# Dropping three of GpSimd's four pacing waits in a message layer, and moving an attention score from TensorE's table to VectorE

## The chip, the cores and the metric

The kernel runs on one core of a Trainium2 chip. The metric is the time of one execution on the device in microseconds. The core has five engines with instruction queues of their own: TensorE (PE, with its weight loads shown as PEld), VectorE (DVE), ScalarE (ACT), GpSimd (POOL), and SyncE (SP), which here only issues transfers. Engines wait for each other by semaphores alone.

## The reference, cut to what matters

Two graph layers over 12,500 nodes with 32 features each, with a layer norm after each. The first layer has 400,000 edges, the second is computed in this kernel over the same edge list.

```
# layer 0, per edge e (source node src[e], target dst[e]):
x    = silu(edge_radial @ W1 + b1)          # 8 -> 64
x    = silu(x @ W2 + b2)                    # 64 -> 64
tpw  = x @ W3 + b3                          # 64 -> 256, four 8x8 blocks per edge
m0   = a * (sum_u hs[src] sh0 W00 + sum_u,i hv[src] sh1 W110 / sqrt(3))
m1   = a * (sum_u hs[src] sh1 W01 + sum_u hv[src] sh0 W10)
agg  = segment_sum(concat(m0, m1), dst) / 4
x    = layernorm(x + h_self + agg)

# layer 1:
s_src, s_dst = x @ attn_w[:32], x @ attn_w[32:]
e     = leaky_relu(s_src[src] + s_dst[dst], 0.01)
alpha = exp(e - segment_max(e)) / segment_sum(exp(...))
x     = layernorm(x + segment_sum(x[src] * alpha, dst))
```

## The kernel before, in words

Edges are sorted by target. Edge number p*3125 + t lies on partition p, column t; a "tile" is one column t of 128 edges.

**The message stage** (about the first 4,700 us) goes over 130 iterations of 24 tiles. An iteration has four groups k = 0..3 (`SLOTS`) of 6 tiles; groups 0 and 1 are half 0, groups 2 and 3 are half 1. All engines run the same loop, two iterations unrolled, each in the order in which its instructions are written; there is no planner.

- TensorE, for each group g: the third layer of g (`layer3`, L595, 6 matmuls into one of two PSUM banks `tpw`, ends with `tpw_ready`), the second layer of g+1 (`layer2`, L585), after k = 1 and k = 3 a one-hot product that fetches one tile's node rows from a table in SBUF (`find_tile`, L604, 14 matmuls), and the first layer of g+2 (`layer1`, L581, ends with `layers_done`). So TensorE is two groups ahead of VectorE.
- ScalarE, for each group: silu after the second layer (`hidden`, L685), at k = 0 and 2 a copy of the gathered rows (`spread_hv`, L698), the one-hots for `find_tile` (L707, L710), some counting work for the first 101 iterations, and last silu after the first layer of g+2 (`first_hidden`, L679, waits for `layers_done`).
- VectorE: two products of the third layer's output with the gathered rows (`product_a`, L953, and `product_b`, L962, which ends with `tpw_used`), their reductions, and the previous iteration's scaling (L992 once per iteration) and scan.
- GpSimd: `gather_again` issues one indirect DMA for each tile whose node rows come from HBM: 6 for k = 0, 5 for k = 1, 6 for k = 2, 5 for k = 3 (L475, tile name `early<-in_x_wide,idx`). In the first 101 iterations one more follows, `gather_dst_row` (`dst_row`). They fill the row slots of the next iteration. What a slot must wait for is `tpw_used`: VectorE is done with that slot's rows. The function has a second wait beside it:

```
pool.wait_ge(tpw_used, it * SLOTS + k - 1)
if k % HALF == 0:
    pool.wait_ge(tpw_ready, it * SLOTS + k - 1)
else:
    pool.wait_ge(layers_done, it * SLOTS + k)
```

That is: before groups 0 and 2 also for TensorE's third layer of the group two before the one gathered for, counted in TensorE's order, and before groups 1 and 3 for the first layer. SyncE refills the inputs and loads the next indices once the gathers of both halves have landed.

**The attention stage** (from about 4,960 to 8,180 us) goes over 125 blocks of 25 tiles. For 17 of them (`GT1`) GpSimd gathers rows of 33 floats (32 features and the score `s_src`) from a table in HBM, `gather_block`; before every fourth gather it waits for `found_ready` of a tile of TensorE's. The other 8 tiles (`PT`) TensorE fetches: `find_rows`, L662, 8 tiles x 7 node batches x 2 splits (the table as high part and low part), each a 128x128 one-hot against `BC` = 14 x 33 = 462 columns. VectorE then picks one of the 14 nodes by a mask product (`keep_one`, L1268) and a reduction (L1276) into `ring`, makes the one-hots for the next block (L1253), and runs the softmax with running maximum (`softmax_block`). All 33 columns, the score among them, come out of the product; `ring[:, k, :, D]` is the score that L1287 reads.

Of the kernel before, what the change touches and what calls it, by code (L numbers as in the profile page):

```python
# [5 lines left out]
ALU = mybir.AluOpType  # L6
ACT = mybir.ActivationFunctionType
AX = mybir.AxisListType.X
# [5 lines left out]
P = 128  # L14
# [37 lines left out]
PA = GT * MUL * 3 * MUL  # L52
GT1 = BT - PT
PC = PT * P
BC = BJ * TW
CHUNKS = ((0, (PT + 1) // 2), ((PT + 1) // 2, PT))
SPLITS = 2
ROUND = 12582912.0
# [20 lines left out]
def build(nc, x, x_wide, x_t, src, src_pe, src_rows, src_pex, src_rowsx, dst, dst_firsts, dst_edges, sh, radial_t, w1, b1, w2, b2, w3, b3, w_self,  # L79
# [17 lines left out]
    with ExitStack() as ctx:  # L97
# [6 lines left out]
        def sem(name):  # L104
            return ctx.enter_context(nc.semaphore(name))
# [53 lines left out]
        def msgs(m, tiles):  # L159
# [70 lines left out]
        picked_at = run_at + run_size  # L230
        picked = [prod_f[:, picked_at + i * BC:picked_at + (i + 1) * BC].rearrange("p (w a) -> p w a", a=BJ)
                  for i in range(2)]

        with ExitStack() as first:
            def sb1(name, shape, dt=F32):
# [12 lines left out]
        with ExitStack() as second:  # L248
            def sb2(name, shape, dt=F32):
                return second.enter_context(nc.sbuf_tensor(name, shape, dt))  # L250

            lows = sb2("lows", [P, NJ * TW], F32R)
            highs = sb2("highs", [P, NJ * TW], F32R)
            hot_f = sb2("hot", [P, NBATCH * PC], F32R)

        xs = xs_f[:, NJ * (TW - D):NJ * TW].rearrange("p (j d) -> p j d", d=D)
# [68 lines left out]
        splits_ready, hot_ready = sem("splits_ready"), [sem(f"hot_ready{i}") for i in range(2)]  # L325
        found_ready, found_used = sem("found_ready"), sem("found_used")
        mask_ready, picked_ready = sem("mask_ready"), sem("picked_ready")
        run_ready, run_stored = sem("run_ready"), [sem(f"run_stored{i}") for i in range(2)]

        decay_ready = sem("decay_ready")  # L330
# [142 lines left out]
        def _(pool):  # L473
# [13 lines left out]

            def gather_again(it, k, m, loads, all_tiles=False):
                pool.wait_ge(tpw_used, it * SLOTS + k - 1)
                if k % HALF == 0:  # L490
                    pool.wait_ge(tpw_ready, it * SLOTS + k - 1)
                else:
                    pool.wait_ge(layers_done, it * SLOTS + k)
                if k == 0:
                    pool.wait_ge(idx_in[m], loads * 16 + 16)
                pool.nop(nofuse=True)
                gather_tiles(m, k, all_tiles)
# [340 lines left out]
        def _(dve):  # L838
# [376 lines left out]
            for b in range(NBATCH):  # L1215
                js = slice(b * BJ, (b + 1) * BJ)
                dve.wait_ge(batch_in[0][b], 16 * BJ)
                link(dve.tensor_tensor(vv[0], agg0[0:P, js, :], bc(has_w[0:P, js]), ALU.mult))
                link(dve.tensor_tensor(vv[1], vv[0], xs[0:P, js, :], ALU.add))
                link(layernorm(h1[0:P, js, 0:D]))  # L1220
                for a, dest in ((0, h1[0:P, js, D:TW].rearrange("p j o -> p (j o)")), (1, tval[0:P, js])):
                    link(dve.tensor_tensor(
                        vv[2], h1[0:P, js, 0:D],
                        attns[0:P, a * D:(a + 1) * D].unsqueeze(1).to_broadcast([P, BJ, D]), ALU.mult))
                    link(dve.tensor_reduce(dest, vv[2], AX, ALU.add))
                dve.sem_inc(h1_ready, 1)
                whole = h1[:, js, :].rearrange("p j w -> p w j")
                hi, lo = (split(s, b).rearrange("p (w j) -> p w j", j=BJ) for s in range(SPLITS))
                link(dve.tensor_copy(hi, whole))
                dve.tensor_tensor(lo, whole, hi, ALU.subtract).then_inc(splits_ready, 1)  # L1230
# [15 lines left out]
            def one_hot(b, n, k, c):  # L1246

                first_tile, end_tile = CHUNKS[c]
                if c == 0:
                    dve.wait_ge(qb_in[k], n * 16 + 16)  # L1250
                dve.wait_ge(found_ready, b * PT + end_tile)
                for g in range(NBATCH):
                    ins = dve.tensor_scalar(hot(c)[:, g, :], qb[k][:, first_tile * P:end_tile * P],  # L1253
                                            slot_of[:, g:g + 1], None, ALU.is_equal)
                ins.then_inc(hot_ready[c], 1)

            def pick(b, n, k):

                edges = bass.ds(b * PT, PT)
                dve.tensor_tensor(mask[:, k, :, :], amod[:, edges].unsqueeze(2).to_broadcast([P, PT, BJ]),  # L1260
                                  iota.unsqueeze(1).to_broadcast([P, PT, BJ]), ALU.is_equal).then_inc(mask_ready, 1)
                dve.wait_ge(mask_ready, b + 1)

                def keep_one(i):
                    dve.wait_ge(found_ready, b * PT + PT + i + 1)
                    if i > 1:
                        dve.wait_ge(picked_ready, b * PT + i - 1)
                    dve.tensor_tensor(picked[i % 2], found[i][:, 0:BC].rearrange("p (w a) -> p w a", a=BJ),  # L1268
                                      mask[:, k, i:i + 1, :].to_broadcast([P, TW, BJ]), ALU.mult).then_inc(found_used, 1)

                keep_one(0)
                for i in range(PT):
                    if i + 1 < PT:
                        keep_one(i + 1)
                    dve.wait_ge(found_used, b * PT + PT + i + 1)
                    dve.tensor_reduce(ring[:, k, GT1 + i, :], picked[i % 2], AX, ALU.add).then_inc(picked_ready, 1)  # L1276
                    if i + 1 == CHUNKS[0][1]:
                        one_hot(b + 1, n + k, 1 - k, 0)
                one_hot(b + 1, n + k, 1 - k, 1)

            def softmax_block(b, pair, k):
                n = b * BLOCK_STEPS
                edges = bass.ds(b * BT, BT)
                top = run[:, k, :, SW - 1]
                dve.wait_ge(ring_in[k], pair * (16 * GT1) + 16 * GT1)
                dve.wait_ge(picked_ready, b * PT + PT)
                dve.tensor_tensor(score[:, 0, :], ring[:, k, :, D], filled[:, edges], ALU.add)\  # L1287
                   .then_inc(block_step, 1)
                dve.wait_ge(block_step, n + 1)
                dve.scalar_tensor_tensor(out=score[:, 1, :], in0=score[:, 0, :], scalar=0.01,  # L1290
                                         in1=score[:, 0, :], op0=ALU.mult, op1=ALU.max)\
                   .then_inc(block_step, 1)

                dve.wait_ge(block_step, n + 2)
                dve.wait_ge(run_stored[k], pair * 16 + 16)
                dve.wait_ge(row0_ready, b + 1)
                dve.tensor_tensor_scan(top[:, 1:], pen[:, edges], score[:, 1, :], top[:, 0:1],
                                       ALU.add, ALU.max).then_inc(block_step, 1)

                dve.wait_ge(block_step, n + 3)  # L1300
                dve.tensor_tensor(diff[:, 0, :], top[:, 0:BT], pen[:, edges], ALU.add)\
                   .then_inc(block_step, 1)
                dve.tensor_tensor(diff[:, 1, :], score[:, 1, :], top[:, 1:], ALU.subtract)\  # L1303
                   .then_inc(block_step, 1)
                dve.wait_ge(block_step, n + 4)
                dve.tensor_tensor(diff[:, 0, :], diff[:, 0, :], top[:, 1:], ALU.subtract)\
                   .then_inc(block_step, 1)
                dve.wait_ge(exp_ready, b + 1)
                for f in range(0, D, MUL):
                    ins = dve.tensor_tensor(acc[:, f:f + MUL, :].rearrange("p f t -> p t f"),  # L1310
                                            acc[:, D, :].unsqueeze(2).to_broadcast([P, BT, MUL]),
                                            ring[:, k, :, f:f + MUL], ALU.mult)
                ins.then_inc(ring_used, 1)
                dve.tensor_copy(run[:, 1 - k, 0, SW - 1:SW], run[:, k, BT, SW - 1:SW]).then_inc(row0_ready, 1)
                dve.wait_ge(ring_used, b + 3)
                dve.wait_ge(decay_ready, b + 1)
                first = acc[:, :, 0]
                dve.scalar_tensor_tensor(out=first, in0=got[1 - k][:, :, BT - 1], scalar=enter1[:, :], in1=first,
                                         op0=ALU.mult, op1=ALU.add).then_inc(added, 1)
                dve.wait_ge(added, b + 1)  # L1320
                for f in range(0, TW, PART):
                    part = slice(f * BT, min(f + PART, TW) * BT)
                    ins = dve.tensor_tensor_scan(got_f[k][:, part], decay_f[:, part], acc_f[:, part], 0.0,
                                                 ALU.mult, ALU.add)
                ins.then_inc(scanned1, 1)
# [132 lines left out]
```

## Time and profile before

| | |
|---|---|
| Times of three runs | 8414.13, 8416.13, 8420.86 us; median 8416.13 |
| Profiled execution | span 8423.6 us, its own time 8425.42 us |
| Busy over the span | PE 80%, PEld 62%, DVE 77%, ACT 33%, POOL 64% |
| Mean granted TensorE clock | 0.888 of full speed |
| DMA | 363 MB in 318,658 packets, 43 GB/s over the span |

The ends of TensorE's matmuls in a profile are modelled from their size; the starts are recorded. A busy share says little by itself here, since the two stages have different limits: the rows below are read by stage.

### The profile page before, as it was taken

To read this page: it belongs to the slowest core of one execution; us is meant where nothing else is said; L and a number is where in the kernel's file an instruction comes from. 1 tells how busy PE (TensorE), PEld (TensorE's weight loads), DVE (VectorE), ACT (ScalarE), POOL (GpSimd) and SP (SyncE) were. 2 spreads that over 40 slices of the span, in tenths; PEclk is the share of its full clock that TensorE was granted. 3 is DMA by queue.
4 is the path that set the end of the run, shared out by engine and by line. 5 is a ranking of instruction groups with operands and counts; after the bars stand their busy time and mean duration, and the time that the engine had idled before them with its cause. 6 is when DMAs were issued, how large, how long until landed. Compare 5 with 4: busy or idle time off the path is not lost.

```text
span 8423.6 us, 93644 instructions
## 1 busy us (share of the span) xinstructions
PE 6705.5 (80%) x26126; PEld 5191.3 (62%) x26126; DVE 6512.7 (77%) x11130; ACT 2820.1 (33%) x4982; POOL 5375.5 (64%) x5400
## 2 busy tenths in 40 slices
PE   6777777777777777777777508999999999999992
PEld 4555555555555555555555407888888888888881
DVE  7888877888878787888787537878787788787874
ACT  4555555555545545544444201111111111111110
POOL 5666666666656666666565566666666666666666
PEclk8888888888888888888888659999999999999996
DMA  2222122222222211211111202222222222222221
GB/s 62 42 41 42 40 41 42 42 42 41 41 39 42 41 41 38 42 39 35 34 33 32 48 18 47 50 51 48 48 53 48 48 48 53 48 48 53 48 48 27
DMA packets 318658, 363.23 MB, mean 43 GB/s; under 512 B 157447, under 2 KB 259511, under 8 KB 317963
## 3 DMA queue, kind: packets, MB, share of 16 engines
q0 software_dynamic: 175840, 136.07, 12.2%
q1 hardware_dynamic: 142794, 226.94, 8.4%
q14 instruction: 19, 0.15, 0.0%
q8 instruction: 5, 0.08, 0.0%
HBM read 251.38 MB, written 111.20 MB: 43 GB/s over the span
## 4 chain that ended last, share of the span: by engine, by line
PE 59%; issue 16%; another core or an unknown queue 9%; DVE 8%; ACT 6%; POOL 1%; DMA 1%; ACTq 0%; DVEq 0%; SPq 0%; POOLq 0%
PE tpw L662 26%; PE tpw L595 12%; PE hid L662 8%; PE hid L604 4%; PE hid L585 4%; PE hid L581 4%; ACT early L685 2%; ACT nearx L707 1%; POOL msgs L475 1%; ACT hid L679 1%; DVE early L974 1%; DVE prod L962 1%; DVE msgs L1023 1%; DVE prod L953 1%
## 5 line engine op out<-in xcount | busy, mean ns | idle before, releaser
L475 POOL DMA_INDIRECT early<-in_x_wide,idx x2870 | 2803.5, 977 | 1793.9 <-issue 1724.5
L475 POOL DMA_INDIRECT prod<-table,idx x2125 | 2180.5, 1026 | 1023.1 <-issue 597.1
L662 PE MATMUL tpw<-highs,hot 128*128 128x462 f32 x5250 | 1993.8, 380 | 78.1 <-issue 62.1
L662 PE MATMUL tpw<-lows,hot 128*128 128x462 f32 x5250 | 1979.3, 377 | 50.9 <-issue 50.3
L595 PE MATMUL tpw<-w3s,early 128*128 128x256 f32 x6252 | 1842.4, 455 | 6.9 <-issue 6.9
L595 PEld LDWEIGHTS tpw<-w3s,early 128*128 128x128 f32 x6252 | 1384.4, 229 | 575.5 <-issue 341.9
L662 PEld LDWEIGHTS tpw<-highs,hot 128*128 128x128 f32 x5250 | 1007.2, 192 | 234.7 <-issue 107.0
L662 PEld LDWEIGHTS tpw<-lows,hot 128*128 128x128 f32 x5250 | 1002.1, 191 | 186.1 <-issue 75.4
L685 ACT ACTIVATE early<-hid,b2s 64x384 f32<-64x384 f32 x1042 | 601.5, 577 | 1008.9 <-PE hid L585 570.1
L581 PE MATMUL hid<-early,w1s 16*128 16x384 f32 x1044 | 546.3, 607 | 485.3 <-ACT early L685 410.0
L585 PE MATMUL hid<-hid,w2s 128*128 128x384 f32 x1042 | 499.2, 563 | 500.2 <-ACT hid L679 274.0
L604 PE MATMUL hid<-x_highs,hotx 128*128 128x448 f32 x1792 | 770.2, 430 | 116.5 <-DVE pickedx L1053 114.1
L815 ACT ACTIVATE big<-diff 128x25 f32<-128x25 f32 x125 | 28.1, 225 | 2384.9 <-DVE diff L1303 1018.0
L935 DVE TENSOR_TENSOR bprod<-hv,sh 128x288 f32<-128x288 f32 (+1 forms) x261 | 121.8, 467 | 891.9 <-ACT hv L698 582.5
L1253 DVE TENSOR_SCALAR hot<-big,bases 128x512 fp32r<-128x512 f32 x1764 | 725.1, 482 | 0.2 <-DVE prod L1243 0.2
L953 DVE TENSOR_TENSOR prod<-tpw,early 128x1152 f32<-128x1152 f32 x521 | 700.3, 1344 | 24.3 <-remote 24.1
L604 PE MATMUL hid<-x_lows,hotx 128*128 128x448 f32 x1792 | 700.5, 391 | 0.0
L962 DVE TENSOR_TENSOR prod<-tpw,hv 128x1152 f32<-128x1152 f32 x521 | 700.1, 1344 | 0.0
L1268 DVE TENSOR_TENSOR prod<-tpw,mask 128x462 f32<-128x462 f32 x750 | 467.6, 637 | 274.7 <-remote 158.3
L662 PE MATMUL hid<-highs,hot 128*128 128x462 f32 x1750 | 656.7, 375 | 9.8 <-issue 9.7
L662 PE MATMUL hid<-lows,hot 128*128 128x462 f32 x1750 | 652.6, 373 | 7.5 <-issue 7.4
L581 PEld LDWEIGHTS hid<-early,w1s 16*128 16x128 f32 x1044 | 170.9, 204 | 737.4 <-issue 476.7
(186 smaller groups left out, 8729.0 us busy)
## 6 DMA issues: line engine op xcount, KB each, us to landing
big<-qrows SPq DMA_DIRECT2D x126, 512.0 KB
scan<-prod SPq DMA_DIRECT2D x125, 425.0 KB
scan<-sums SPq DMA_DIRECT2D x130, 384.0 KB
early<-in_x_wide,idx POOLq DMA_INDIRECT x2870
prod<-table,idx POOLq DMA_INDIRECT x2125
qbx<-qx SPq DMA_DIRECT2D x131, 128.0 KB
early<-in_radial_t SPq DMA_DIRECT2D x262, 48.0 KB
sh<-in_sh SPq DMA_DIRECT2D x131, 48.0 KB
```

The source lines that it names most:

```text
L475: return pool.indirect_dma_start(out=dest, out_offset=None, in_=source, in_offset=bass.IndirectOffsetOnAxis(ap=index, axis=0))
L581: pe.matmul(hid[:, 0, 0:HC], w1s[:, :], rad[:, k, :], start=True, stop=True).then_inc(layers_done, 1)
L585: pe.matmul(hid[:, 0, 0:HC], w2s[:, :], hid1[:, :], start=True, stop=True).then_inc(layer2_done, 1)
L595: mm = pe.matmul(tpw_v(b)[:, t, :], hid2[:, b, at:at + P], w3s[:, :], start=True, stop=True)
L604: mm = pe.matmul(hid[:, 1, 0:BX], hotx[m][:, g, h * P:(h + 1) * P], x_split(s, g), start=g == 0 and s == 0, stop=g == NBATCH - 1 and s == ...
L662: mm = pe.matmul(found[i][:, 0:BC], hot(c)[:, g, at:at + P], split(s, g), start=g == 0 and s == 0, stop=g == NBATCH - 1 and s == SPLITS - 1)
L685: ins = act.activation(hid2[0:HR, b, half * HC:(half + 1) * HC], hid[units, 0, 0:HC], ACT.Silu, bias=b2s[units, :])
L935: dve.tensor_tensor(bprod[:, 0:tiles, :, :], hv[:, h, 0:tiles, :].rearrange("p t (i u) -> p t i u", i=3), sh1.rearrange("p o i t -> p (o t ...
L953: dve.tensor_tensor(prod_a[b].rearrange("p (t w u) -> p t w u", t=GT, w=MUL), w[:, :, 0:3 * MUL * MUL].rearrange("p t (w u) -> p t w u", w ...
L962: dve.tensor_tensor(prod_b[b].rearrange("p (t i w u) -> p t i w u", t=GT, i=3, w=MUL), w[:, :, 3 * MUL * MUL:].rearrange("p t (w u) -> p t ...
L1253: ins = dve.tensor_scalar(hot(c)[:, g, :], qb[k][:, first_tile * P:end_tile * P], slot_of[:, g:g + 1], None, ALU.is_equal)
L1268: dve.tensor_tensor(picked[i % 2], found[i][:, 0:BC].rearrange("p (w a) -> p w a", a=BJ), mask[:, k, i:i + 1, :].to_broadcast([P, TW, BJ]) ...
```

## The change

Two edits that have nothing to do with each other.

In the message stage GpSimd's second wait stays for k = 0 alone, with the same value as before; for k = 1, 2 and 3 only the wait for `tpw_used` is left.

In the attention stage TensorE's node table and its products have 32 columns per node instead of 33 (462 columns become 448). The score of the 8 tiles that TensorE fetches is computed by VectorE instead: after the eighth tile is picked, one product of the 8 x 32 picked features with the attention weights and one sum over the 32 features, written into column `D` of the ring. The softmax block waits for that (`found_scored`) in place of `picked_ready`. The table in HBM and GpSimd's gathers keep 33 columns.

```diff
-BC = BJ * TW
+BC = BJ * D
...
+        by_attn_at = picked_at + 2 * BC
+        by_attn = prod_f[:, by_attn_at:by_attn_at + PT * D].rearrange("p (t d) -> p t d", d=D)
+        assert by_attn_at + PT * D <= 4 * PA
...
-            highs = sb2("highs", [P, NJ * TW], F32R)
+            highs = sb2("highs", [P, NJ * D], F32R)
...
+        by_attn_ready, found_scored = sem("by_attn_ready"), sem("found_scored")
...
             def gather_again(it, k, m, loads, all_tiles=False):
                 pool.wait_ge(tpw_used, it * SLOTS + k - 1)
-                if k % HALF == 0:
-                    pool.wait_ge(tpw_ready, it * SLOTS + k - 1)
-                else:
-                    pool.wait_ge(layers_done, it * SLOTS + k)
+                if k == 0:
+                    pool.wait_ge(tpw_ready, it * SLOTS - 1)
                 if k == 0:
                     pool.wait_ge(idx_in[m], loads * 16 + 16)
                 pool.nop(nofuse=True)
...
-                whole = h1[:, js, :].rearrange("p j w -> p w j")
+                whole = h1[:, js, 0:D].rearrange("p j w -> p w j")
...
                     dve.tensor_tensor(picked[i % 2], found[i][:, 0:BC].rearrange("p (w a) -> p w a", a=BJ),
-                                      mask[:, k, i:i + 1, :].to_broadcast([P, TW, BJ]), ALU.mult).then_inc(found_used, 1)
+                                      mask[:, k, i:i + 1, :].to_broadcast([P, D, BJ]), ALU.mult).then_inc(found_used, 1)
...
-                    dve.tensor_reduce(ring[:, k, GT1 + i, :], picked[i % 2], AX, ALU.add).then_inc(picked_ready, 1)
+                    dve.tensor_reduce(ring[:, k, GT1 + i, 0:D], picked[i % 2], AX, ALU.add).then_inc(picked_ready, 1)
...
                 one_hot(b + 1, n + k, 1 - k, 1)
+                dve.wait_ge(picked_ready, b * PT + PT)
+                dve.tensor_tensor(by_attn, ring[:, k, GT1:, 0:D],
+                                  attns[:, 0:D].unsqueeze(1).to_broadcast([P, PT, D]), ALU.mult).then_inc(by_attn_ready, 1)
+                dve.wait_ge(by_attn_ready, b + 1)
+                dve.tensor_reduce(ring[:, k, GT1:, D], by_attn, AX, ALU.add).then_inc(found_scored, 1)
...
-                dve.wait_ge(picked_ready, b * PT + PT)
+                dve.wait_ge(found_scored, b + 1)
                 dve.tensor_tensor(score[:, 0, :], ring[:, k, :, D], filled[:, edges], ALU.add)\
                    .then_inc(block_step, 1)
```

## Rows read from the trace of the kernel before

**Rows 1.** The page's chain that ended last, shares by engine.
```profile
PE 59%; issue 16%; another core or an unknown queue 9%; DVE 8%; ACT 6%; POOL 1%; DMA 1%; ACTq 0%; DVEq 0%; SPq 0%; POOLq 0%
```

**Rows 2.** Windows: stretch, its length, busy us (instructions) by engine, clock, DMA.
```profile
200.00:4500.00 4300.00, 3313.99 (x10975) 2272.32 (x10974) 3468.65 (x4297) 2175.22 (x4062) 2650.51 (x2715) 0.87 0.20 40
5500.00:8000.00 2500.00, 2391.62 (x11007) 2094.57 (x11007) 2010.11 (x4817) 353.38 (x441) 1712.19 (x1672) 0.98 0.23 50
```

**Rows 3.** Waits, whole span: us in total, times, longest us.
```profile
ACT hid L679 <- remote: 703.7, 135, 7.8
DVE bprod L935 <- ACT hv L698: 582.5, 150, 9.1
```

**Rows 4.** Timeline of one message iteration: start us, us, instruction [idle before <-releaser].
```profile
3015.66 0.95 POOL L475 DMA_INDIRECT early<-in_x_wide,idx  x1 [4.91 <-issue]
...
3024.17 1.35 DVE L962 TENSOR_TENSOR prod<-tpw,hv 128x1152 f32<-128x1152 f32 x1
...
3025.41 0.91 PE L581 MATMUL hid<-early,w1s 16*128 16x384 f32 x2
...
3028.30 0.95 POOL L475 DMA_INDIRECT early<-in_x_wide,idx  x1 [0.30 <-issue]
...
3030.58 1.33 DVE L962 TENSOR_TENSOR prod<-tpw,hv 128x1152 f32<-128x1152 f32 x1
3031.21 0.58 ACT L679 ACTIVATE hid<-hid,b1s 128x384 f32<-128x384 f32 x1 [7.39 <-remote]
...
3032.06 0.95 POOL L475 DMA_INDIRECT early<-in_x_wide,idx  x1 [2.81 <-issue]
...
3050.74 0.95 POOL L475 DMA_INDIRECT early<-in_x_wide,idx  x1 [3.52 <-issue]
```

**Rows 5.** Timeline of two later iterations without a pause before k = 2.
```profile
4027.34 0.95 POOL L475 DMA_INDIRECT early<-in_x_wide,idx  x1 [9.79 <-issue]
...
4066.19 0.94 POOL L475 DMA_INDIRECT early<-in_x_wide,idx  x1 [9.91 <-issue]
...
4390.29 0.95 POOL L475 DMA_INDIRECT early<-in_x_wide,idx  x1 [8.04 <-issue]
...
4400.99 0.58 ACT L679 ACTIVATE hid<-hid,b1s 128x384 f32<-128x384 f32 x1 [2.86 <-issue]
...
4418.35 0.95 POOL L475 DMA_INDIRECT early<-in_x_wide,idx  x1 [0.30 <-issue]
...
4421.54 1.36 DVE L953 TENSOR_TENSOR prod<-tpw,early 128x1152 f32<-128x1152 f32 x1 [2.95 <-remote]
...
4430.65 0.94 POOL L475 DMA_INDIRECT early<-in_x_wide,idx  x1 [11.35 <-issue]
```

**Rows 6.** Line L992, in every second iteration: first and last start.
```profile
L992 DVE TENSOR_TENSOR early<-early,sh x65: 947/949/987, 126.8 to 4738.8; 128x768 f32<-128x768 f32 x65
```

**Rows 7.** Pieces of the chain: back-to-back matmuls of 462 and of 448 columns.
```profile
3043.28 2.81 PE hid L604 x14
...
5105.57 17.72 PE tpw L662 x84
```

**Rows 8.** Groups by line and form: busy us, mean ns, idle before.
```profile
L1276 DVE TENSOR_REDUCE prod<-prod 128x33 f32<-128x462 f32 x1000 | 613.6, 624 | 0.0
L1268 DVE TENSOR_TENSOR prod<-tpw,mask 128x462 f32<-128x462 f32 x750 | 467.6, 637 | 274.7 <-remote 158.3 <-PE hid L662 55.6 <-PE tpw L662 29.2
L1053 DVE TENSOR_TENSOR pickedx<-hid,maskx 128x448 f32<-128x448 f32 x256 | 157.6, 616 | 0.0
L1061 DVE TENSOR_REDUCE early<-pickedx 128x32 f32<-128x448 f32 x256 | 155.5, 608 | 0.0
L935 DVE TENSOR_TENSOR bprod<-hv,sh 128x288 f32<-128x288 f32 x260 | 121.5, 467 | 891.9 <-ACT hv L698 582.5 <-issue 234.7 <-DMA sh<-in_sh 74.4
L475 POOL DMA_INDIRECT early<-in_x_wide,idx x2870 | 2803.5, 977 | 1793.9 <-issue 1724.5 <-PE hid L581 31.1 <-DVE prod L962 19.0
L475 POOL DMA_INDIRECT prod<-table,idx x2125 | 2180.5, 1026 | 1023.1 <-issue 597.1 <-remote 185.1 <-PE tpw L662 181.6
```

## The prediction

> **What bounds the kernel now.** I read the chain that ended last first. TensorE has 59% of it, and 9% is "another core or an unknown queue", odd on a single core [rows 1]. The windows then part two stages. In the message stage no engine is full: over 4,300 us VectorE is busy 3,469, TensorE 3,314, and the clock is 0.87. In the attention stage TensorE is: 2,392 of 2,500 us at clock 0.98 [rows 2]. There 11,007 matmuls at 112 a block are 98.3 blocks, 25.44 us each, of which VectorE is idle (2,500 - 2,010) / 98.3 = 5.0 us.
>
> The waits say what the odd 9% is: ScalarE's L679 waits 703.7 us for "remote", 135 times, 5.2 us each, about once per iteration [rows 3]. L679 waits only for TensorE's first layer. The timeline of one iteration shows it. TensorE's first layer (L581) starts at 3025.41 and takes 0.91, so it is over at 3026.32. But ScalarE's L679 starts at 3031.21, and GpSimd's gather before k = 2, which waits for the third layer that follows L581, at 3032.06 [rows 4]. Nothing else releases them: TensorE's signals arrive late, that of the first layer by 4.9 us, and together. When do they come? GpSimd had issued 11 gathers from 3015.66 to 3028.30 + 0.95 = 3029.25; L679 starts 1.96 us after that. I went through the timeline of all iterations with L581 and L679 side by side: of 127, L679 is late by more than 4 us in 90, again about 1.9 us after the last gather of the run, and on time in 37 (of the first 99, which have `gather_dst_row`, 78 late and 21 on time; of the last 28, 12 and 16). Signals given in the first five gathers of a run are on time, those given after the eighth mostly late, those after the eleventh nearly always. I take it as this kernel's rule, without knowing its cause: while GpSimd issues indirect DMAs back to back, TensorE's signals get stuck after about 10 us and come out when the run has drained. So the pauses in GpSimd's run are worth something, and the change removes the one before k = 2.
>
> **Message stage.** Before groups 1 and 3 the removed wait ends no idle time: gathers follow each other at 1.25 us. The value for k = 0 is unchanged. What counts is k = 2: GpSimd idles 3032.06 - 3029.25 = 2.81 us there [rows 4]. Without that wait, k = 2 needs VectorE's third `product_b` counted from that run's iteration, started 3024.17, over at 3025.52, and k = 3 the one started 3030.58, over at 3031.91. GpSimd reaches k = 2 at 3015.66 + 11 x 1.25 = 3029.4 and k = 3 at 3036.9. Both are met, so the two runs of 11 and 12 gathers become one of 23 (22 after iteration 100). That lasts 28.75 us from the start S of the run, and the drain ends at S + 28.75 + 1.9 = S + 30.65.
>
> The trace has two such runs, where the wait before k = 2 happened to be met in time: from 4027.34 and 4390.29. They go without a pause, the second to 4418.35 + 0.95. Start of run to start of next is 38.85 and 40.36 us, against 35.08 for 3015.66 to 3050.74 [rows 4, 5], and 36.0 us mean: 128 iterations from 126.8 to 4738.8 [rows 6]. In both L679 was on time (4400.99), but the third layer's signal was then stuck until the drain, and VectorE's L953 waited until 4421.54, 2.2 us after the last gather [rows 5]. So a merged run costs (38.85 + 40.36) / 2 - 36.0 = 3.6 us where L679 is on time, and 1.25 more for the 23rd gather: 4.9.
>
> Where L679 is late, it is stuck from S + 10.7 on. Before, release to next run start was 3050.74 - 3031.2 = 19.6 us: second layer, silu, `spread_hv`, VectorE's products, the third layer that k = 0 waits for. That stretch now begins at S + 30.65, so the iteration takes 50.2 us, +14.2 (22 gathers: 49.0, +13.0). VectorE, idle from S + 16.3, covers nothing.
>
> Behind GpSimd's waits only gathers are queued, and who waits for them (`spread_hv`) is not waiting for their landing now. So an earlier landing gives 0; at most the 2.81 us before k = 2 could come back each iteration, 360 us.
>
> Which of the two cases? I keep the shares of now, since S and what TensorE and VectorE do after it keep their order: 78 x 14.2 + 21 x 4.9 + 12 x 13.0 + 16 x 3.6 = 1,108 + 103 + 156 + 58 = 1,425 us. Bounds: all on time 99 x 4.9 + 28 x 3.6 = 586; all late 99 x 14.2 + 28 x 13.0 = 1,770.
>
> The Trainium skill, Perfetto Trace Analysis, in its section on what the profiler's window captures for TensorE, says that a matmul's end is computed from its size, and that the signal is pushed only when PSUM has acknowledged the write. By that rule the gap between 3026.32 and 3031.21 could be matmuls that really ended late, and GpSimd would have no part in it; that is the second rival below. Rows 4 and 5 speak against it: the same matmuls let L679 go at once in the iteration of 4400.99, at the same place in the run (10.7 us after its start).
>
> **Attention stage.** TensorE: 84 matmuls of 462 columns take 17.72 us, 0.2110 each, and 14 of 448 columns 2.81, 0.2007 [rows 7]. That saves 0.0103 x 112 = 1.15 us a block, 144 us if TensorE alone set the pace. VectorE: eight products fall from 637 to 616 ns and eight reductions from 624 to 608, 0.30 us less [rows 8]; a product and a reduction of 256 elements are added. No row has that size; the product of 288 takes 467 [rows 8], so two at up to 0.47, and two handovers of about 0.1: +1.1, net +0.8 us. It lies after the picks and before the softmax, in 5.0 us of idle time a block. If that cover were gone it would cost 0.8 x 125 = 100 us. GpSimd: 17 gathers at 1.026 + 0.30 are 22.5 us a block [rows 8], about what TensorE's block becomes (112 x 0.2007 = 22.5), so the engines touch, and GpSimd's pauses for `found_ready` shrink with the faster tiles, which lets its runs grow. Half of the gain: -70 us, between -144 and +100. The splits of the table are seven shorter copies ahead of the stage, and narrower operands there are worth under 1 us.
>
> GpSimd's gathers take 1,026 ns here and 977 in the message stage [rows 8]. The Trainium skill, GPSIMD Engine Reference, Key points, gives a reason that speaks against the change: GpSimd shares its SBUF interfaces with VectorE, and a VectorE instruction with two SBUF inputs contends with it. The added product is one. By that rule a gather could be held up by 0.47 us, 58 us in 125 blocks, inside the bound above.
>
> **The sum.** The profiled execution's own time is 8425.4 us (span 8423.6). + 1,425 - 70 = 9,780. That execution is 9.3 above the median of 8416.13, so 9,770.
>
> **Rivals.**
> 1. Mild: the long run shifts the phase so that L679 is on time as in the two natural cases. For it: both natural long runs were on time, and so was the run after them. Against: in the first 99 iterations 79% are late. Time: 8,416 + 586 - 70 = 8,930.
> 2. The late signals have nothing to do with the length of GpSimd's run, only with `find_tile` ahead of them. Then the merged run costs nothing and attention gives its 70 to 144, perhaps with part of the 2.81 us an iteration: 8,416 - 70 = 8,350, down to about 8,000. For it: each late signal follows the 14 matmuls, and the two natural long runs are only two. Against: the release follows the end of the gathers, not that of the matmuls. This is the other side; it decides if L679 starts under 5 us after L581 in the new trace although the run goes on.
> 3. The pauses don't go: `product_b` comes later than GpSimd in the new steady state, so `tpw_used` splits the run by itself. Then the message stage stays within +-1 us an iteration; with attention 8,220 to 8,480. Against: margins of 3.9 and 5.0 us [rows 4].
>
> **How the numbers follow.** Forecast 0.60 (9,400 to 10,150 of its own), mild 0.23 (8,700 to 9,300), rival 2 0.11, rival 3 0.06. Two executions of this kernel differ by up to 0.08%, so 0.2% (17 us) can be told from no change. Faster by more: rival 2 and half of 3, 0.13. Within: 0.02. Slower: 0.85. The range leaves out the faster side and the very top: 8,700 to the all-late bound, 8,416 + 1,770 + 100 = 10,290.
>
> **What would show it.** Right: GpSimd's idle time before the seventh to twelfth gather gone; runs of 22 and 23; L679's wait for "remote" near 20 us a time in most iterations; intervals of L992 of 50 and 41 us; TensorE's clock in the message stage below 0.87, as it idles; a step of 0.20 us for L662 and blocks near 24.9 us. Wrong: L679 released in the middle of a run; runs still split before k = 2; intervals under 37 us.

## The result and the profile after

The changed kernel takes 9817.78 us (median of 4 runs, 9802.88 to 9851.71) against 8415.13 for the kernel before (4 runs, 8413.39 to 8420.86). The ratio is 1.167, with a 95% interval of 1.164 to 1.170: slower by a sixth, 48 us above the forecast of 9,770.

The chain that ended last, in the page of the changed kernel, answers to [rows 1]:

```profile
PE 46%; issue 20%; another core or an unknown queue 19%; DVE 8%; ACT 5%; DVEq 0%; ACTq 0%; DMA 0%; SPq 0%
```

"Another core or an unknown queue" was 9% and is 19%, on a single core. The windows, with the columns of [rows 2], say in which stage:

```profile
200.00:4500.00 4300.00, 2530.87 (x8403) 1725.16 (x8402) 2658.63 (x3299) 1695.42 (x3190) 2037.23 (x2104) 0.79 0.16 31
7000.00:9300.00 2300.00, 2145.49 (x9981) 1919.11 (x9980) 1873.29 (x4542) 320.41 (x401) 1557.17 (x1517) 0.97 0.23 49
```

In the message stage each engine runs 21 to 23% fewer instructions in the same 4,300 us, and the clock falls from 0.87 to 0.79. In the attention stage 9,981 matmuls are 89.1 blocks of 112, 25.8 us each, where they were 25.4. So almost the whole loss is in the message stage. From the first to the last matmul of the third layer it takes 6,070.5 us instead of 4,712.7, which is +1,358 of the 1,402 between the two profiled executions. The attention stage, measured the same way, is 3,219.0 instead of 3,175.2, and the remaining 536 us are unchanged within 1 us.

One iteration shows how. Timeline of the changed kernel, columns of [rows 4]; L583 is TensorE's first layer, L587 the second, L681 and L687 are ScalarE's silus behind them (L679 and L685 before):

```profile
2973.69 0.95 POOL L479 DMA_INDIRECT early<-in_x_wide,idx  x1 [14.32 <-PE tpw L597]
...
2983.45 0.91 PE L583 MATMUL hid<-early,w1s 16*128 16x384 f32 x2
...
2987.57 0.95 POOL L479 DMA_INDIRECT early<-in_x_wide,idx  x1 [0.30 <-issue]
...
2999.24 0.58 ACT L681 ACTIVATE hid<-hid,b1s 128x384 f32<-128x384 f32 x1 [17.40 <-remote]
2999.88 1.65 PE L587 MATMUL hid<-hid,w2s 128*128 128x384 f32 x2 [12.74 <-issue]
...
3001.33 0.94 POOL L479 DMA_INDIRECT dst_row<-in_dst,row_i  x1 [0.31 <-issue]
3006.39 1.17 ACT L687 ACTIVATE early<-hid,b2s 64x384 f32<-64x384 f32 x2 [6.56 <-remote]
...
3008.17 0.46 DVE L937 TENSOR_TENSOR bprod<-hv,sh 128x288 f32<-128x288 f32 x1 [18.22 <-ACT hv L700]
...
3025.81 0.95 POOL L479 DMA_INDIRECT early<-in_x_wide,idx  x1 [23.53 <-issue]
```

GpSimd issues its 23 gathers from 2973.69 to 3002.27 without a pause; the gather at 2987.57, the twelfth, had 2.81 us of idle time ahead of it before. TensorE's first layer is over at 2984.36 (2983.45 + 0.91). Its signal reaches ScalarE at 2999.24, 14.9 us later. The second layer is over at 3001.53, and its signal reaches L687 at 3006.39, 4.9 us later and 4.1 after the last gather. Then comes the stretch that no gather covers, until the third layer releases the next run. The iteration takes 52.1 us. The second layer's 1.65 us are a price of the idle time as well: TensorE had stood still for 12.74 us, and windows around the two places give its granted clock in the column behind POOL, full (2.4 GHz) at 2983.4 and half (1.2 GHz) at 2998.5:

```profile
2983.40:2984.40 1.00, 1.00 (x4) 0.41 (x4) 1.00 (x3) 0.00 (x0) 0.70 (x1) 1.00 0.19 23
...
2998.50:3001.60 3.10, 1.65 (x2) 0.50 (x2) 0.00 (x0) 0.58 (x1) 2.18 (x4) 0.50 0.12 16
```

Waits over the whole span, columns of [rows 3]:

```profile
POOL early L479 <- issue: 2245.6, 2800, 25.2
DVE bprod L937 <- ACT hv L700: 1788.3, 202, 18.3
ACT early L687 <- remote: 1187.9, 118, 16.4
ACT hid L681 <- remote: 890.9, 56, 22.3
```

L681 is late less often than L679 was (56 of these waits instead of 135) but by 15.9 us instead of 5.2. The second silu, which before had 54 such waits of 5.5 us on average, has 118 of 10.1 us.

### The profile page after: what moved, and what is told of

Read it like the earlier page. It is cut to its first block, busy times and chain, and to the rows that moved or that the text cites. A ratio compares the mean times of both kernels' runs of the same rounds, so it can differ in the third digit from the quotient of the medians.

```text
span 9825.9 us, 93830 instructions
## 1 busy us (share of the span) xinstructions
PE 6667.5 (68%) x26126; PEld 5203.4 (53%) x26126; DVE 6578.7 (67%) x11380; ACT 2820.0 (29%) x4982; POOL 5365.7 (55%) x5400
## 4 chain that ended last, share of the span: by engine, by line
PE 46%; issue 20%; another core or an unknown queue 19%; DVE 8%; ACT 5%; DVEq 0%; ACTq 0%; DMA 0%; SPq 0%
PE tpw L664 21%; PE hid L664 7%; PE tpw L597 7%; PE hid L606 6%; PE hid L587 3%; PE hid L583 2%; ACT early L687 2%; ACT nearx L709 2%; DVE early L976 1%; ACT hid L681 1%; DVE pickedx L1055 1%; ACT hv L700 1%; DVE hot L1255 1%; DVE early L945 1%
## 5 line engine op out<-in xcount | busy, mean ns | idle before, releaser
L479 POOL DMA_INDIRECT prod<-table,idx x2125 | 2187.6, 1029 | 1058.2 <-issue 585.9
L664 PE MATMUL tpw<-highs,hot 128*128 128x448 f32 x5250 | 1946.0, 371 | 51.4 <-issue 32.5
L664 PE MATMUL tpw<-lows,hot 128*128 128x448 f32 x5250 | 1951.4, 372 | 40.2 <-issue 39.9
L597 PE MATMUL tpw<-w3s,early 128*128 128x256 f32 x6252 | 1787.4, 444 | 8.4 <-issue 7.1
L597 PEld LDWEIGHTS tpw<-w3s,early 128*128 128x128 f32 x6252 | 1349.5, 223 | 576.7 <-issue 357.5
L583 PE MATMUL hid<-early,w1s 16*128 16x384 f32 x1044 | 570.3, 631 | 1358.9 <-ACT early L687 703.6
L587 PE MATMUL hid<-hid,w2s 128*128 128x384 f32 x1042 | 535.2, 600 | 970.6 <-issue 616.8
L687 ACT ACTIVATE early<-hid,b2s 64x384 f32<-64x384 f32 x1042 | 601.6, 577 | 1984.7 <-remote 1187.9
L583 PEld LDWEIGHTS hid<-early,w1s 16*128 16x128 f32 x1044 | 179.5, 214 | 1632.7 <-issue 1489.9
L587 PEld LDWEIGHTS hid<-hid,w2s 128*128 128x128 f32 x1042 | 196.6, 214 | 1098.0 <-issue 657.4
L664 PE MATMUL hid<-lows,hot 128*128 128x448 f32 x1750 | 679.6, 388 | 62.6 <-issue 62.5
L664 PE MATMUL hid<-highs,hot 128*128 128x448 f32 x1750 | 676.0, 386 | 67.5 <-issue 66.8
```

The source lines that it names most:

```text
L479: return pool.indirect_dma_start(out=dest, out_offset=None, in_=source, in_offset=bass.IndirectOffsetOnAxis(ap=index, axis=0))
L583: pe.matmul(hid[:, 0, 0:HC], w1s[:, :], rad[:, k, :], start=True, stop=True).then_inc(layers_done, 1)
L587: pe.matmul(hid[:, 0, 0:HC], w2s[:, :], hid1[:, :], start=True, stop=True).then_inc(layer2_done, 1)
L597: mm = pe.matmul(tpw_v(b)[:, t, :], hid2[:, b, at:at + P], w3s[:, :], start=True, stop=True)
L664: mm = pe.matmul(found[i][:, 0:BC], hot(c)[:, g, at:at + P], split(s, g), start=g == 0 and s == 0, stop=g == NBATCH - 1 and s == SPLITS - 1)
L687: ins = act.activation(hid2[0:HR, b, half * HC:(half + 1) * HC], hid[units, 0, 0:HC], ACT.Silu, bias=b2s[units, :])
```

## Experiments

Each run is told by its edit against the changed kernel, and timed beside the kernel before on the same chip. "Stage" is the message stage as above.

**The two halves of the change, each alone.** First the waits with the 33 columns of before, then the columns with the waits of before:

```diff
 # e1: the changed waits, BC = BJ * TW and the score by TensorE as before
 # e2: the changed columns, and
-                if k == 0:
-                    pool.wait_ge(tpw_ready, it * SLOTS - 1)
+                if k % HALF == 0:
+                    pool.wait_ge(tpw_ready, it * SLOTS + k - 1)
+                else:
+                    pool.wait_ge(layers_done, it * SLOTS + k)
```

> The kernel before with GpSimd's waits as in the changed one, TensorE's table still 33 columns wide. Theory (merged runs of gathers hold TensorE's signals back): all of the loss in the message stage is here. The changed trace has its message stage 1,358 us longer, so 8,415 + 1,358 = 9,770 to 9,780, with iterations of 50 to 52 us alternating with 42 to 44. If the columns or the new VectorE work in the attention stage were part of the message stage's loss by some coupling: under 9,700.

> The 32-column table and the score by VectorE alone, GpSimd's waits as before. Message stage as before (36.0 us an iteration). Attention stage: the changed trace has it 44 us longer (3,219 against 3,175 us), against the predicted 70 us shorter. If that holds by itself: 8,455 to 8,465. If the attention stage's loss came from anything the message stage left behind (phase, clock): 8,345 to 8,415.

Measured: e1 9810.27 us beside 8420.11, ratio 1.165 (1.162 to 1.168), stage 6,029 us. e2 8427.95, ratio 1.0009 (1.0000 to 1.0018), stage 4,660 us. The waits are the whole loss: e1 came out 30 us above its forecast. The columns are worth nothing that can be told from zero: +8 us, 0 to +15. That lies between the two bands given for e2, so it decides for neither. In its trace the message stage is 52 us shorter than in the trace of the kernel before, though the code of that stage is the same, and the attention stage 44 us longer. The kernel before has no trace from this chip, so how the +8 divides between the stages is open.

**Which of the waits removed.** The third layer's before k = 2 put back, then the first layer's before k = 1 and k = 3 instead:

```diff
 # e3
-                if k == 0:
-                    pool.wait_ge(tpw_ready, it * SLOTS - 1)
+                if k % HALF == 0:
+                    pool.wait_ge(tpw_ready, it * SLOTS + k - 1)
 # e4, beside the wait for k == 0
+                if k % HALF == 1:
+                    pool.wait_ge(layers_done, it * SLOTS + k)
```

> The changed kernel with the wait for the third layer back for k = 2 as well; only the waits for the first layer (k = 1 and 3) are gone. Theory: the pause before k = 2 is the one that counts, runs of 11 and 12 return, and the time is that of the columns alone, about 8,460, ratio to before 1.003 to 1.008. Rival (the odd groups' waits also hold something up): above 8,600.

> The changed kernel with the waits for the first layer (k = 1 and 3) back, the one for the third layer before k = 2 still gone. Theory: k = 2 starts at once, so the run goes to 17 gathers; the signal that k = 3 waits for (the first layer given after about 18 us in the run) is itself late, so GpSimd stops there after 17 gathers, the run drains, and the signals come out at S + 17 x 1.25 + 1.9 = S + 23.2 instead of S + 30.65. Late iterations about 50.2 - 7.4 = 43 us plus the second run's share, on-time ones 38 to 40: 41 us mean, 8,415 + 5 x 127 + 44 = about 9,100. Rival (the odd waits do nothing, they are met before): 9,820 as the changed kernel.

Measured: e3 8435.54, ratio 1.0017 (1.0008 to 1.0026), below its band of 1.003 to 1.008; its runs are of 11 and 12 gathers again, but for two of 22. e4 9277.14, ratio 1.102 (1.099 to 1.104); its runs are of 17 and 6, or of 5, again but for two of 22. So the wait before k = 2 is the one that counts. e4 came out 2% above its forecast. The time follows the longest run: 12 gathers 8,436, 17 gathers 9,277, 23 gathers 9,810.

**Is it the wait for TensorE, or the pause?** Here GpSimd waits for its own gathers to land, and for nothing that TensorE does:

```diff
 # e5
+                if k == 2:
+                    pool.wait_ge(rows_in[0], rows_until(it))
 # e6: that, and before k = 1 and k = 3
+                if k % HALF == 1:
+                    pool.wait_ge(rows_in[k // HALF], rows_until(it) - 16 * (GT if all_tiles else GT - 1))
```

> The changed kernel with a pause of another kind before k = 2: GpSimd waits until its own gathers for k = 0 and 1 have landed, and for nothing of TensorE's. Theory (signals are held while GpSimd gathers back to back, whoever ends the run): runs of 11 and 12 with a pause of about 2.4 us, first-layer signal released as before, 36 us an iteration, 8,410 to 8,450. Rival (it is TensorE's wait itself, the order it forces, that kept the stage fast, for instance by keeping GpSimd from running ahead): near 9,800.

> The changed kernel with such a pause before k = 1, 2 and 3: runs of 6, 5, 6 and 5 (6 with dst_row), none past 7.5 us. Theory: no signal is ever held, ScalarE's L679 starts at once in all iterations, the 5 us wait goes; GpSimd needs 23 x 1.25 + 3 x 1.3 = 32.7 us plus its wait for k = 0, VectorE 29 us, so 33 to 35 us an iteration and 8,100 to 8,350, below the kernel before. Rival (length of the run doesn't matter, any 20 us of gathers with TensorE busy hold signals): L679 as late as before and, with more pauses, 8,450 to 8,700.

Measured beside 8390.41: e5 8326.57, ratio 0.991 (0.989 to 0.994). e6 8391.79, ratio 1.000 (0.998 to 1.002). One wait for its own landings gives back all that the changed kernel lost (1,400 us on the first chip; it was not run on this one), and 64 us more. It misses its forecast on the good side: e5 beats the kernel before as well as the changed one. e6 misses too, on the other side. Its waits, in two answers, one by engine ScalarE and one by GpSimd:

```profile
ACT early L691 <- remote: 371.2, 94, 16.1
...
POOL early L479 <- DMA early<-in_x_wide,idx: 434.9, 308, 2.4
```

With runs of 5 or 6 gathers, and in most iterations one of 12, the signal of the first layer after the first find came over 2 us late in 1 of 127 iterations, against 69 in e5. The second layer's was late instead, 93 times, but by 2.8 us only. Yet the mean iteration takes 35.9 us. In the 95 iterations whose last group runs into the next k = 0 without a pause (the runs of 12), GpSimd itself is the bound: 23 gathers at 1.25 are 28.75, and three pauses of about 2.3 make 35.7. A pause has a price, and at three an iteration it eats what the signals on time give.

**Is it the matmuls of the find, or the bytes of the gathers?**

```diff
 # e7: find_tile's 14 matmuls become 2
-                for g in range(NBATCH):
+                for g in range(1):
 # e8: gathers of the message stage fetch 64 rows instead of 128
+                    p = P if all_tiles else P // 2
+                    gather(rows[0:p, k, t, :], x_wide[:, :], idx[0:p, m, k * GT + t:k * GT + t + 1])\
```

> The changed kernel with find_tile cut from 14 matmuls to 2 (one node batch of seven: part of the rows of two tiles in 24 is left out of the sum). Theory (length of GpSimd's run): TensorE's queue is 2.4 us shorter twice an iteration, so the first layer's signal is given at S + 8.3 instead of S + 10.7 and is more often on time, but the later ones are still held until the drain at S + 30.65: 40 to 48 us an iteration, 9,000 to 9,800. Rival (the 14 matmuls ahead are what delays the signals): L679 on time everywhere, 34 to 36 us, 8,250 to 8,450.

> The changed kernel with every gather of the message loop (from the second iteration on) fetching rows for 64 of the 128 partitions (the other half keeps old rows), so half the descriptors and bytes, the same number of instructions. If GpSimd's instruction time of 0.95 + 0.30 us is per instruction, runs still last 28.75 us. Then: if what holds the signals is the descriptors or packets in the DMA queue, L679 is on time and the iteration falls to about 36 us or less, 8,400; if it is GpSimd's being busy for long, it stays at 45 to 47 us, 9,700 to 9,820. If the instruction gets shorter with fewer descriptors, the runs shorten too and the two are told apart by how late signals are at a given time in the run.

Measured: e7 9350.05, ratio 1.113 (1.103 to 1.123). e8 10502.21, ratio 1.251 (1.243 to 1.258). In e7 the first layer after the find ends 8.6 us into the run (median) instead of 10.7, and its signal is never over 2 us late. But the second layer's is over 2 us late 128 times, by a median of 8.1 us, and the third layer's 135 times, by 8.2. ScalarE's waits of e7, for the second layer:

```profile
ACT early L687 <- remote: 1583.4, 124, 20.6
```

That ends rival 2: the find only decides which signal falls into the time when they are held. e8 was forecast at no worse than the changed kernel, and this was wrong. Timeline of e8, columns as above:

```profile
3322.62 0.90 POOL L479 DMA_INDIRECT early<-in_x_wide,idx  x1 [23.20 <-PE tpw L598]
...
3332.37 0.91 PE L584 MATMUL hid<-early,w1s 16*128 16x384 f32 x2
...
3354.94 0.58 ACT L682 ACTIVATE hid<-hid,b1s 128x384 f32<-128x384 f32 x1 [22.17 <-remote]
...
3375.18 0.90 POOL L479 DMA_INDIRECT early<-in_x_wide,idx  x1 [24.75 <-issue]
```

With half the rows GpSimd takes about as long to issue a gather (0.90 us, one in 1.20, against 0.95 and 1.25), and the run is still of 23 gathers. In the iteration shown the signal is held for 21.7 us, from 3333.28 to 3354.94, and one is held in 126 of 127 iterations; in the changed kernel it was 63. So fewer rows do not shorten the hold; with as many gathers back to back it is longer. Why the halved ones hold it longer is open. (e7 and e8 leave out part of the rows, so their output is wrong and only their time counts.)

**How short may the pause be?** GpSimd fills a tile that nobody reads, once or twice, and waits for nobody:

```diff
 # e11; e12 has the fill twice
+                if k == 2:
+                    pool.wait_ge(padded, it)
+                    pool.nop(nofuse=True)
+                    pool.memset(pad[:, :], 0.0).then_inc(padded, 1)
```

> The changed kernel with one pause put back before slot 2 that waits for nobody: GpSimd fills a spare tile of 128x1024 (an estimate from its fill of 128x128 in 0.22 us and of 128x1 in 0.10: some 1.1 us, so about 1.4 us between two gathers). Theory A, the held signals come out in any gap of GpSimd's gathers that is longer than a micro-second: runs of 11 and 12 again, one short pause, 8250 to 8400 us, at or under the kernel with the wait for its own landings (8327). Theory B, they come out only about 1.7 to 1.9 us after a run's last gather, as in every kernel so far: the gap is too short, GpSimd loses 1.4 us per iteration for nothing, and the time stays at 9700 to 9950 us.

> The same with two such fills, an estimate of 2.2 us and 2.5 us between two gathers, as long as the pause for its own landings (median 2.5 us). It waits for nobody. Theory A and theory B both: 8300 to 8450 us, since 2.5 us is over 1.9. Rival: what lets the signals out is that GpSimd stands in a wait, not the length of the gap; an engine that fills a tile in that time isn't waiting, and the time stays at 9700 to 9950 us, as for a gap that is too short.

Measured: 7823.53 and 7823.75 us, but beside 7908.29 for the kernel before, which took 8390 to 8420 in every earlier run. Both ratios are 0.989 (0.988 to 0.991). The chip is another one, and on it nothing is held. Chain of e11 and its waits of ScalarE:

```profile
PE 56%; DVE 21%; issue 14%; POOL 4%; ACT 4%; DMA 1%; DVEq 0%; ACTq 0%; SPq 0%; POOLq 0%
```

```profile
ACT early L694 <- PE hid L594: 1132.8, 521, 6.0
...
ACT hid L688 <- PE hid L590: 438.2, 260, 3.0
```

The "another core or an unknown queue" of the chain is gone, and so is every wait for "remote" of the two silus. Of TensorE's signals recorded in the message stage of that trace, none comes more than 0.015 us after its instruction's end; nine of ten iterations take 34.0 to 34.3 us. The runs could not say how short a pause may be. If nothing else sets that chip apart, the held signals cost the kernel before some 490 us, 6%, on the others. That is argued: the kernel before was timed there, and has no trace from that chip. One more thing differs: that trace has 118,000 records of semaphore updates, the traces from the other chips 42,000 to 53,000, with many missing. Whether the recording itself has a part in the holds was not tested. The two that follow ask both questions again:

> The changed kernel itself, nothing edited, beside the kernel before on whatever chip the run gets. The last two runs came to a chip where the kernel before takes 7908 us instead of 8390 to 8420, and where no signal of TensorE in the profile comes later than 0.02 us after its instruction's end. Theory (the whole loss is the held signals): if this chip is of that kind (before near 7908), the changed kernel takes 7780 to 7900, as the one with the fill of a tile (7824), and is not slower than before; if it is of the kind of the first runs (before near 8400), 9800 to 9850 again. Rival (the loss is in the kernel's own waits: slots gathered too early, rows overtaken, the order on ACT): about 9200 to 9350 beside 7908, and 9800 beside 8400.

> The kernel with one fill of a 128x1024 tile before slot 2 (0.97 us in the profile, so some 1.3 us between two gathers), run again since on the chip of the last runs no signal was held and it could tell nothing. If before is near 8400 here: theory A (any gap over a micro-second lets the signals out) 8250 to 8400; theory B (they come out 1.7 to 1.9 us after the last gather) 9700 to 9950. If before is near 7908: 7824 again, and the question of the shortest pause stays open.

They ran on yet another chip, where before takes 8399.87: e13, the changed kernel itself, 9549.75, ratio 1.136 (1.132 to 1.140), and e14, the kernel of e11, 9530.41, ratio 1.135 (1.132 to 1.138). e13 is below its band of 9,800 to 9,850, so the size of the loss is not the same on every chip that holds signals. e14's timeline:

```profile
3027.23 0.94 POOL L481 DMA_INDIRECT early<-in_x_wide,idx  x1 [14.48 <-PE tpw L604]
...
3036.98 0.91 PE L590 MATMUL hid<-early,w1s 16*128 16x384 f32 x2
...
3040.81 0.97 POOL L504 MEMSET pad<- 128x1024 f32 x1
3041.94 1.05 POOL L481 DMA_INDIRECT early<-in_x_wide,idx  x1 [0.17 <-issue]
...
3042.83 0.58 ACT L688 ACTIVATE hid<-hid,b1s 128x384 f32<-128x384 f32 x1 [7.45 <-remote]
3043.46 0.91 PE L594 MATMUL hid<-hid,w2s 128*128 128x384 f32 x2 [2.79 <-ACT hid L688]
...
3052.72 1.17 ACT L694 ACTIVATE early<-hid,b2s 64x384 f32<-64x384 f32 x2 [9.31 <-remote]
```

and the same place in e5, on another chip that holds them:

```profile
2419.10 0.91 PE L585 MATMUL hid<-early,w1s 16*128 16x384 f32 x2
...
2424.96 0.58 ACT L683 ACTIVATE hid<-hid,b1s 128x384 f32<-128x384 f32 x1 [7.46 <-remote]
2425.24 0.94 POOL L479 DMA_INDIRECT early<-in_x_wide,idx  x1 [2.32 <-issue]
2425.59 0.91 PE L589 MATMUL hid<-hid,w2s 128*128 128x384 f32 x2 [2.80 <-ACT hid L683]
2426.55 1.16 ACT L689 ACTIVATE early<-hid,b2s 64x384 f32<-64x384 f32 x2 [1.00 <-PE hid L589]
```

In both the first layer's signal comes about 2.0 us after the first run's last gather. In e5 GpSimd had paused until then (2.32 us), and the second layer's signal passes at once: L589 ends at 2426.50, L689 starts at 2426.55. In e14 GpSimd had gone on after 1.13 us, and the second layer's signal is held: L594 ends at 3044.37, L694 starts at 3052.72, 8.3 us later. Theory A's time (8,250 to 8,400) is refuted. B's band is missed by 170 us, as e13 missed its own by 250. The short gap does do something: the signal that is held comes out about 2 us after the last gather, as B says, although the next run has begun. But the next signal is held. Over the whole message stage, of TensorE's signals recorded in the first 5 us of a run, 121 of 268 are over 1 us late in e14 and 0 of 316 in e5. e12's longer gap without a wait was not run where signals are held, so that a gap alone is enough stays open.

## Why the prediction was right

**The wait before k = 2 and the merged run: right.** The runs are of 23 gathers (99 times) and 22 (29 times), with no pause before k = 2, as `product_b` is early enough. e3 shows that this wait alone is the difference, and e5 that its worth was the pause: a wait for GpSimd's own gathers, which has nothing to do with TensorE, does as well.

**Late iterations: the price right, its mechanism only in part.** 51.2 us on average where L681 is late, against 50.2 forecast. But the step "stuck until the drain" does not hold in a long run: of 63 late signals 57 came out before the last gather ended, as in the iteration shown, 3.03 us before it. What brings the iteration to 51 us all the same is a second hold. The signal of the second layer is caught in the same run and comes out after it. The forecast added 19.6 us to S + 30.65; here L687 starts at S + 32.70 and the next run 19.4 us after that.

**Iterations on time: mis-sized.** The two natural cases gave +4.9 us for a run of 23 gathers; the 63 on-time iterations take 42.4 us on average, +6.4 over 36.0. Two cases were few, and more were at hand: in the trace of the kernel before, 16 further iterations pause only 0.93 to 1.03 us before k = 2 and take 38.1 us on average, and in all 16 L679 is on time.

**The shares: mis-sized.** I kept 90 late iterations of 127 (read as over 4 us late; over 4 us are 83 of them, over 2 us all 90). There were 63, since late and on-time iterations now alternate. What parts them is narrow: in the kernel before, all 90 late signals were given 10.65 us or more after the start of their run and 34 of the 37 on time before that. In the changed kernel 62 of the 63 late ones were given after 10.64 us, and 62 of the 64 on time before. By measured values the stage is 63 x (51.2 - 36.0) + 63 x (42.4 - 36.0) = 1,361 us longer, as measured (1,358), where 1,425 was forecast. The errors, too many late ones and too cheap ones, went against each other. With the gain of 70 us that did not come, they leave the forecast 48 us off, so its closeness is in part luck. Two of its own signs did not come either: L679's waits (now L681's) are near 16 us, not 20, and in half of the iterations, not in most; and the blocks of the attention stage take 25.8 us, not 24.9.

**Attention: the gain did not come.** I took half of 144 us as gain. The profiled executions differ by +44, and e2 by +8 (0 to +15) over the whole kernel. But the same attention code takes 3,171 us in e5 and e13, on two other chips, so the +44 is no larger than what chips differ by. The pieces of the chain in the changed kernel answer to [rows 7]:

```profile
6460.82 17.22 PE tpw L664 x84
...
6505.32 5.74 PE hid L664 x28
```

A matmul of 448 columns comes every 0.2050 us here, against 0.2110 for 462 and the 0.2007 that I took from the find of the message stage. That is 0.0060 x 112 = 0.67 us a block instead of 1.15, 84 us in all. More than that is given back in waits. Of the 14,000 steps between matmuls of this stage, 786 are over 0.3 us, 505 us together; before 527 were, with 333 us. VectorE's added operations cost 0.84 us a block, a little under the 0.94 estimated, and the handover between the two takes 0.03 us (median), where the sum had 0.1:

```profile
L1286 DVE TENSOR_REDUCE prod<-prod 128x8 f32<-128x256 f32 x122 | 51.5, 422 | 4.2
L1283 DVE TENSOR_TENSOR prod<-prod,attns 128x256 f32<-128x256 f32 x122 | 51.1, 419 | 0.0
L1278 DVE TENSOR_REDUCE prod<-prod 128x32 f32<-128x448 f32 x979 | 586.4, 609 | 0.0
L1270 DVE TENSOR_TENSOR prod<-tpw,mask 128x448 f32<-128x448 f32 x736 | 447.8, 622 | 226.8 <-remote 118.7 <-PE hid L664 51.2 <-PE tpw L664 18.9
```

"Remote" stands ahead of L1270 as well: signals are held in this stage too. Where none are, in e11, TensorE sets the pace and hides VectorE's work: 123 of 124 blocks of the same code take 22.96 us, 112 x 0.2050, and the stage 2,872 us instead of 3,219. So the faster matmuls are real, and where signals are held their gain goes into waits. That the 85 us by which e11 beats the kernel before there are these 84 is likely, and not shown apart. The gathers of this stage went from 1,026 to 1,029 ns, where one gather in 17 held up by 0.47 us would have added 28 ns to the mean. By the rule of the Trainium skill, GPSIMD Engine Reference, Key points, such a contention could have shown here, and the trace has no sign of it.

**Rivals.** Rival 1, the mild one, described half of the iterations. Rival 2 fell with e7 and e5, rival 3 with the runs of 23. The rule of the Trainium skill, Perfetto Trace Analysis (what the profiler's window captures for TensorE), that a matmul's end is only modelled could have made these signals late on paper alone. The trace does not agree: e5 and e14 have the same matmuls ahead of L683 and L688, and the one lets the next signal through and the other does not.

**The chip, which no step considered.** The prediction took the held signals for a property of the kernel. Four of the five sets of runs show them, one does not. The changed kernel was not run there. As e11 differs from it only by the fill and is 1.1% faster than before on that chip, I would expect no loss there; that is argued, not shown.

## What to carry to other kernels

A wait that looks idle can be what keeps other engines' signals moving: before removing one, look in the timeline at what is released in the microseconds behind it. Where indirect DMAs go out back to back for over 10 us and the waits for TensorE end with "remote" on a single core, try one wait for the gathers' own landing (about 2.3 us) in the middle of the run; here three an iteration gave nothing. Time such a change on more than one chip, since here the chips differ by 6%, and the best version by 1%.

## What the runs showed of the hardware

- TensorE's semaphore signals given more than about 10 us into a run of back-to-back indirect DMAs arrive late. Where the first layer's after the first find is over 2 us late, the median is 4.8 us with runs of 11 and 12 (kernel before, 90 times), 14.2 with 22 and 23 (changed kernel, 63 times; 9.1 in e13 on another chip), and 21.5 with as many gathers of 64 rows (e8, 126 times). Of those recorded in the first 5 us of a run none is over 1 us late in the traces of the kernel before, the changed kernel and e5. VectorE's and ScalarE's pass: of those recorded behind `product_b` and the first silu in the changed kernel's trace (381 and 348), none is over 0.013 us late. A quarter or more of these records are missing where signals are held. The cause inside the chip is open.
- A gap of 2.3 us between gathers, spent waiting for their landing, ended it (e5). After one of 1.13 us the held signal came out, and the next one was held (e14).
- One chip of those used shows none of it: before takes 7,908 us there instead of 8,390 to 8,420.
- A gather of 64 rows takes GpSimd as long to issue as one of 128, within 5% (0.90 and 0.95 us).
- Back-to-back matmuls of 448 columns came every 0.2007 us in the find of the message stage and every 0.2050 in the table of the attention stage; why is open.
- The best version run is e5, 0.991 of the kernel before where signals are held. On the chip without holds the kernel with a fill in its place gave 0.989.
